# Attention on one NeuronCore: the broadcast of the inverse softmax sums moves from SyncE's queue to the end of GpSimd's batch, the reciprocals from step 8 to step 6

## The reference, cut to what matters

```python
q = x @ W_q; k = x @ W_k; v = x @ W_v
latent_kv = (k + v) @ W_down_kv
k_rec, v_rec = latent_kv @ W_up_k, latent_kv @ W_up_v        # per head
scores = einsum('bhqd,bhkd->bhqk', qh, k_rec) / sqrt(d)
scores = scores * decay
attn = softmax(scores, axis=-1)
out = einsum('bhqk,bhkd->bhqd', attn, v_rec) @ W_o
h = h + out
```

## Time and profile before

| | |
|---|---|
| median of 3 runs | 1879.0 us (1874.41 to 1879.68) |
| the profiled execution | 1886.12 us, its span 1883.9 us |
| mean granted TensorE clock | 0.95 |
| busy: PE, DVE, ACT, POOL | 1676.9, 1217.3, 934.9, 943.4 us (89%, 65%, 50%, 50%) |
| DMA queues | SP's (hardware) 26.4% of 16 engines' span, GpSimd's (software) 11.9% |

### The profile page before, as it was taken

The page is one execution under the profiler, slowest core; times in us unless marked ns, Lnnn a source line. Parts: engine busy times, 40 slices in busy tenths (PEclk is TensorE's granted clock), DMA queues, the critical chain, the costliest instruction groups (busy, mean ns, idle before and its releaser), DMA issues.

```text
span 1883.9 us, 47126 instructions
## 1 busy us (share of the span) xinstructions
PE 1676.9 (89%) x15406; PEld 1246.6 (66%) x15406; DVE 1217.3 (65%) x3822; ACT 934.9 (50%) x2157; POOL 943.4 (50%) x945
## 2 busy tenths in 40 slices
PE   6875888888888888769999869999999999999997
PEld 5873566666666666447777637777777777777775
DVE  2884777787878778665778655555555555555551
ACT  4444666665666666435223554444444444444442
POOL 3772334334343343363223144666666666666665
PEclk9996999999999999979999869999999999999999
DMA  5532544544454454333110052434343333343422
GB/s 184 174 100 62 122 112 123 124 113 123 116 127 117 112 127 115 95 100 79 30 34 26 27 174 83 100 100 101 101 101 101 101 100 98 101 101 101 101 34 28
DMA packets 174164, 186.71 MB, mean 99 GB/s; under 512 B 113401, under 2 KB 148729, under 8 KB 167929
## 3 DMA queue, kind: packets, MB, share of 16 engines
q1 hardware_dynamic: 147192, 141.19, 26.4%
q0 software_dynamic: 26880, 44.36, 11.9%
HBM read 134.59 MB, written 50.44 MB: 98 GB/s over the span
## 4 chain that ended last, share of the span: by engine, by line
PE 56%; SPq 18%; DMA 8%; issue 7%; DVE 5%; POOL 3%; ACT 2%; DVEq 0%; POOLq 0%; ACTq 0%
PE psum L1755 26%; PE psum L1772 13%; SPq L474 10%; PE psum L1620 6%; DMA inverse_sums<-arena 5%; PE psum L1640 4%; SPq L468 3%; SPq L517 3%; POOL hidden L590 1%; POOL arena L595 1%; DMA arena<-k_halves 1%; PE psum L1735 1%; PE psum L1492 1%; ACT arena L758 1%; DVE arena L1132 1%
## 5 line engine op out<-in xcount | busy, mean ns | idle before, releaser
L1755 PE MATMUL psum<-arena,hidden 128*128 128x376 f16 x3072 | 494.0, 324 | 0.9 <-DVE arena L1368 0.9
L657 POOL TENSOR_TENSOR arena<-arena 128x376 f16<-128x376 f32 x320 | 314.6, 985 | 355.1 <-ACT arena L758 353.8
L1755 PEld LDWEIGHTS psum<-arena,hidden 128*128 128x128 f16 x3072 | 301.3, 98 | 189.5 <-issue 2.6
L1132 DVE CUSTOM_DVE_ANT_0 arena<-psum,constants 128x188 f32<-128x188 f32 x768 | 238.3, 347 | 146.2 <-PE psum L1447 140.1
L758 ACT ACTIVATE arena<-arena 128x376 f16<-128x376 f32 (+5 forms) x610 | 283.8, 473 | 61.5 <-DVE arena L1304 45.7
L976 ACT ACTIVATE arena<-psum 128x376 f32<-128x376 f32 x256 | 123.7, 483 | 343.1 <-PE psum L1755 343.1
L612 POOL TENSOR_TENSOR arena<-arena 128x376 f16<-128x376 f32 x128 | 113.7, 897 | 356.0 <-ACT arena L758 353.4
L807 ACT ACTIVATE arena<-psum 128x376 f32<-128x376 f32 x384 | 183.6, 480 | 164.6 <-PE psum L1461 162.9
L1378 DVE SCALAR_TENSOR_TENSOR arena<-psum,arena 128x376 f32<-128x376 f32 x256 | 140.7, 549 | 181.1 <-ACT arena L976 179.6
L1772 PE MATMUL psum<-hidden,arena 128*128 128x256 f16 (+1 forms) x2304 | 256.6, 273 | 0.0
L758 ACT ACTIVATE arena<-psum 128x188 f32<-128x188 f32 (+7 forms) x457 | 176.1, 398 | 160.0 <-PE psum L1492 58.2
(11 more groups left out here) (158 smaller groups left out, 2668.9 us busy)
## 6 DMA issues: line engine op xcount, KB each, us to landing
arena<-e_g SPq DMA_DIRECT2D x16, 1024.0 KB
arena<-e_u SPq DMA_DIRECT2D x16, 1024.0 KB, 5.1
arena<-e_d SPq DMA_DIRECT2D x16, 1024.0 KB, 4.7
arena<-x_t SPq DMA_DIRECT2D x32, 376.0 KB, 3.5
weighed<-arena POOLq DMA_DIRECT2D x32, 376.0 KB, 4.1
arena<-q_halves SPq DMA_DIRECT2D x192, 47.0 KB, 2.4
arena<-k_halves SPq DMA_DIRECT2D x96, 94.0 KB, 2.6
arena<-q_halves SPq DMA_DIRECT2D x96, 94.0 KB, 2.3
```

The costliest lines, as they stand in the source:

```text
L657: nc.gpsimd.tensor_tensor(dst, f, hi, ALU.subtract).then_inc(ready, 1)
L1132: last = nc.vector.tensor_tensor_reduce(out=SC[i % 2 * 2 + u], in0=SB[i % 2][:, u * S:(u + 1) * S], in1=C[:, C_DECAY + t * S:C_DECAY + (t ...
L1755: last = mm(bank[2 * (s % 2) + i][:, 0:CHUNK], w_, a, start=n == 0, stop=n == 5)
```

## The change

The four broadcast DMAs leave SP's batch and stand at the end of GpSimd's, behind `dense_heads`; the wait for `rs_out` goes with them, and the wait for `on_ready` is no longer written, since `dense_heads` ahead of it has it. `invert` moves from step 8 to step 6 of DVE's batch.

```diff
@@ sync engine, spread_halves
                 write(k_dram, b + 3, KS2, kl_ready, k_out)
-                if valid(c):
-                    sp.wait_ge(rs_out, 16 * c + 16)
-                    hold(sp)
-                    at_least(sp, on_ready, c)
-                    hold(sp)
-                    heads = r_dram[:, :].rearrange("(j g) n -> g j n", g=4)
-                    for g in range(4):
-                        sp.dma_start(RD[64 * (g % 2):64 * (g % 2) + 64, g // 2 * S:(g // 2 + 1) * S],
-                                     heads[g].unsqueeze(1).broadcast_to((4, HD, S))).then_inc(rd_in, 16)
@@ gpsimd
+            def spread_inverse(c):
+                if valid(c):
+                    pool.wait_ge(rs_out, 16 * c + 16)
+                    hold(pool)
+                    heads = r_dram[:, :].rearrange("(j g) n -> g j n", g=4)
+                    for g in range(4):
+                        nc.gpsimd.dma_start(RD[64 * (g % 2):64 * (g % 2) + 64, g // 2 * S:(g // 2 + 1) * S],
+                                            heads[g].unsqueeze(1).broadcast_to((4, HD, S))).then_inc(rd_in, 16)
+
@@ gpsimd, batch
                 dense_heads(b - 1)
+                spread_inverse(b - 1)
@@ vector engine, batch
-                    elif n == 8:
+                    elif n == 6:
                         invert(b - 1)
```

## The result

The changed kernel took 1807.5 us (median of 4 runs, 1803.3 to 1809.1) against 1876.7 us for the kernel before (4 runs): a ratio of 0.963, 95% interval 0.960 to 0.965. In a later session, over 5 runs, it was 1806.7 us and 0.959 (0.958 to 0.961); the kernel before took about 1883 us there, and 1884 and 1885 us in the two other sessions of the experiments, so ratios to it are what is compared between sessions. 1803 us had been forecast, in a range of 1784 to 1836.

What follows compares the result with a forecast made beforehand. SP's queue and one wait in it were taken as the bound. 27 batches, each shrinking from 19.51 to 16.6 us, less 2.5 us at the end, save 76 us: median 1879.0 becomes 1803 us, range 1784 to 1836.

Steps and rivals of the forecast that it cites:

- The bound: Steady attention: SP's queue and its wait for the inverses' landing set the pace, 19.51 us a batch.
- SP's 14.2 us: SP's need per batch after the change: 19.5 us less 5.3 us for the wait and the broadcasts' stretch.
- PE's 16.6 us: PE's own time from step 6 to step 6 without the wait for k, taken as the new batch time.
- the nine distances at full clock: Nine of 21 step-6 distances on PE, less the wait: 16.55 to 16.70 us, without stretches at 1.2 GHz.
- the stretches at 1.2 GHz: Slower matmul pairs on PE, 0.52 us instead of 0.33, soon after step-6 waits; expected to go with the wait.
- the mean over all 21 distances: Rival: slow clock stays, from the mix of matmuls; 17.45 us a batch, 53 us saved, 1826 us; chance 0.18.
- The covers: Slack in step 6's batch: KX lands at +11.8, needed at +16.6; GpSimd free at +8.3, needed at +11.3.
- The reciprocals: DVE's inversion moves 4 us ahead, still 0.43 us; could give back up to that a batch, kept for the range.
- The end: Last division of the attention comes 2.5 us later, behind the four broadcasts issued on GpSimd.
- The sum: 27 batches x (19.51 - 16.6) = 78.6 us, less 2.5 at the end: 76 us saved.

Runs made afterwards that it cites:

- the fastest kernel: Changed kernel with DVE's row statistics moved from step 11, and the moments from step 0, to steps 2, 3 and 4: 1785.0 us, 0.948 of the kernel before.
- the kernel with step 8: Changed kernel with the reciprocals left in step 8, so only the broadcasts move to GpSimd: 1809.3 us, 0.960 of the kernel before.
- sixteen issues: Changed kernel with each broadcast on GpSimd cut in four, the same bytes: 1870.6 us, 0.993 of the kernel before.

## Why the prediction was right, point by point

**The bound.** SP's queue was it, as read from the chain and from the wait for k in each step 6. Taking away its wait, its issues or both moves the time in that order, and moving the reciprocals alone does not.

**SP's 14.2 us.** This term was mis-sized. It took the wait and the issues off the whole loop, as if all that was left were issues. The landing of q, which the DMA view before had with 3.9 us, had been hidden under the wait for the inverses and the broadcasts and came out: SP's loop is about 15.5 us, in the fastest kernel 521.66 - 506.00 = 15.7 in one batch. That this did no harm is luck: PE's 16.6 us happen to be longer. Had PE needed 14.5 us, the forecast would have been about a microsecond a batch too low.

**PE's 16.6 us.** 16.68 measured. Taking the nine distances at full clock, less the wait, was the right reading, and both halves came true: the 1.9 us of waiting went, and so did the stretches at 1.2 GHz. With the mean over all 21 distances, 17.45 us, the forecast would have been 1826.

**The covers.** All counted from the start of step 6, forecast and measured: the low part of k ready +2.7 and +3.0; first read +3.8 and +4.6 (the landing of q again); KX issued +9.6 and +10.3; inverses landed +5.3 and +5.0; one broadcast issue 0.62 and 0.60 us; GpSimd free +8.3 and +7.4 (the start of 0.4 us that I had added was not needed); low part of x due +11.3 and +11.4. From GpSimd the broadcasts landed 3.5 us after their issue (median, DMA view), and the division that needs them starts at 514.55, 6.8 us after the last issue ended, so this landing is hidden. The Trainium skill (DMA: Bandwidth & Descriptors, Issuing engine by pattern) calls the Sync path generally faster; for these broadcasts no run here shows it, since the view has no landing for them from SP.

**The reciprocals.** That they would give back up to 0.43 us a batch was kept for the range and did not come: 16.68 us, and 16.67 in the kernel with step 8 (350.05 us over 21 batches). The cover they add was not needed either: 2.5 us were left without it.

**The end.** 2.5 us more were forecast, and it became 0.9 us shorter. From the reads of the weighed values to the last division it grew by 0.7 us (4.8 to 5.6), since the division began 1.9 us after the last issue had ended, and not 3.6 us as behind the reads of the weighed values before; the rest of the end got shorter by 1.6, whose cause is not shown.

**The sum.** Steady saving 2.91 us a batch forecast, 2.74 measured over the 27: the first four of them, which have the entry into the hardware loop among them, saved less than the others ((296.11 - 215.24) - (285.30 - 214.28) = 9.9 us for four). 27 x 2.74 = 74.1, with 3.4 us from the rest 77.4; the forecast had 76. That these two are so close is in part luck: the steady saving was taken 4.5 us too large (78.6 against 74.1), and the rest 5.9 us too small (2.5 us lost against 3.4 gained). The median fell by 69 us in the first session and by 77 in the later one, since the kernel before itself ran 7 us apart.

## What to carry to other kernels

Here a queue that issued all the time was the bound, even though every engine showed idle time. Moving a wait, with what hangs on it, to an idle queue gained down to the next bound, and the distance between two stalls at full clock, less the stall, gave that bound ahead of time. It holds as long as the idle time of the other queue lasts, which sixteen issues used up. Before the length of a wait is subtracted from a loop, ask what it covered (here another landing of almost 4 us). And an edit is to be judged again behind every other: moving DVE's statistics was worth 0.2% before this change and 1.2% behind it.

## What the runs showed that I had not expected

The landing of q, 3.9 us in the kernel before, showed in hardly any wait there (3 waits, 5.5 us in the whole span) and came out as SP's wait when the wait ahead of it was taken away: 14.5 us in 410 in the changed kernel, 23.3 in 350 with the issues kept on SP. A plain broadcast of 47 KB costs GpSimd's queue 0.60 us to issue, 23.5 KB the same, and a quarter (16 partitions) 0.48. Half-speed stretches behind waits of PE of 1.6 to 3.1 us cost about 1.45 us each in the kernel before, and disappear with the waits.
